# Attention and a quantized gated FFN on one core: the small shift product on GpSimd, and five steps placed elsewhere in the order

## The reference

```
xn  = (x - mean) / sqrt(var + 1e-5)            over the 128 features
out = x + attention(xn) + ffn(xn)

attention: q = xn Wqa Wqb (16 heads of 8), k, v = xn Wkva Wkvb (4 heads of 8), rope on q and k,
           causal softmax(q k / sqrt(8)) v, then Wout and a bias
ffn:       h = silu(Q(xn) Q(Wgate)') * (Q(xn) Q(Wup)'), 352 wide;  Q(h) Q(Wdown)'
Q:         blocks of 16: scale = max|.| / 6, each value rounded to the nearest of
           0, 0.5, 1, 1.5, 2, 3, 4, 6 with its sign, times the scale
```

## Time and profile before

| | |
|---|---|
| median of 3 runs | 790.27 us (788.24 to 791.44) |
| the profiled execution | 788.24 us |
| its span in the profile | 785.8 us |
| TensorE busy | 718.4 us (91%) |
| VectorE busy | 627.7 us (80%) |
| GpSimd busy | 588.6 us (75%) |
| ScalarE busy | 535.9 us (68%) |
| DMA queue | 74.25 MB, 35.1% of 16 engines |
| granted TensorE clock, mean | 0.991 of full speed |

### The profile page before, as it was taken

One profiled execution on the slowest core, in us unless ns is written; L12 is line 12 of the kernel. 1 busy time (PEld: TensorE's weight loads), 2 busy tenths in 40 slices (PEclk: granted clock), 3 DMA queues, 4 the chain that ended last, 5 costly groups with the idle time before them and its releaser, 6 DMA issues.

```text
span 785.8 us, 18291 instructions
## 1 busy us (share of the span) xinstructions
PE 718.4 (91%) x6453; PEld 440.8 (56%) x6453; DVE 627.7 (80%) x1424; ACT 535.9 (68%) x1154; POOL 588.6 (75%) x630
## 2 busy tenths in 40 slices
PE   2467899999999999999999999999999999999886
PEld 1233455665656565665656565665656565665443
DVE  6569888889798888989798888989798888878412
ACT  2213676867777777867777777877777777777772
POOL 4533597878879797868889797878788797856662
PEclk9999899999999999999999999999999999999999
DMA  4432224334334433344334334243334333241111
GB/s 111 108 77 82 67 76 109 93 106 113 99 93 117 103 114 97 94 106 113 97 94 119 104 109 105 89 117 104 96 99 126 94 117 95 77 115 46 57 50 49
DMA packets 84885, 75.41 MB, mean 96 GB/s; under 512 B 28627, under 2 KB 66868, under 8 KB 84796
## 3 DMA queue, kind: packets, MB, share of 16 engines
q1 hardware_dynamic: 84796, 74.25, 35.1%
HBM read 40.38 MB, written 27.25 MB: 86 GB/s over the span
## 4 chain that ended last, share of the span: by engine, by line
PE 62%; DVE 15%; ACT 7%; POOL 6%; issue 4%; DMA 3%; SPq 2%; POOLq 0%; DVEq 0%; ACTq 0%
PE pv_ps L1159 16%; PE exp_ps L1137 12%; PE max_ps L1122 8%; DVE neg_max L732 7%; PE misc_ps L1183 5%; PE max_ps L1123 5%; PE misc_ps L1220 5%; ACT P L958 3%; PE misc_ps L1191 3%; PE misc_ps L1208 3%; PE misc_ps L1218 2%; POOL P L555 2%; PE misc_ps L1169 1%; DVE h_mag L694 1%; PE misc_ps L1187 1%
## 5 line engine op out<-in xcount | busy, mean ns | idle before, releaser
L732 DVE TENSOR_REDUCE neg_max<-max_ps 128x1 f32<-128x512 f32 (+3 forms) x768 | 430.4, 593 | 88.2 <-PE max_ps L1123 86.1
L958 ACT ACTIVATE P<-exp_ps 128x512 f32<-128x512 f32 x512 | 294.7, 599 | 164.0 <-PE exp_ps L1137 163.0
L1137 PE MATMUL exp_ps<-Q,K 128*128 128x512 bf16 (+3 forms) x1024 | 243.4, 301 | 10.2 <-ACT P L958 6.8
L1122 PE MATMUL max_ps<-K,Q 128*128 128x384 bf16 (+2 forms) x768 | 198.9, 278 | 20.1 <-DMA Kd<-K 10.5
L1123 PE MATMUL max_ps<-Kd,Q 128*128 128x128 bf16 x1024 | 190.7, 220 | 1.4 <-DVE neg_max L732 1.2
L555 POOL TENSOR_SCALAR_AFFINE_SELECT P<-P 128x512 f32<-128x512 f32 x256 | 161.7, 667 | 30.6 <-ACT P L961 30.6
L1159 PE MATMUL pv_ps<-P,V 128*32 128x512 f32 (+3 forms) x2048 | 163.9, 438 | 1.2 <-POOL P L555 0.8
L1122 PEld LDWEIGHTS max_ps<-K,Q 128*128 128x128 bf16 x768 | 75.6, 99 | 97.6 <-DVE neg_max L732 53.8
L1123 PEld LDWEIGHTS max_ps<-Kd,Q 128*128 128x128 bf16 x1024 | 99.0, 100 | 42.5 <-issue 22.7
L1137 PEld LDWEIGHTS exp_ps<-Q,K 128*128 128x128 bf16 x1024 | 79.6, 98 | 48.0 <-ACT P L958 26.4
L586 POOL TENSOR_TENSOR h<-gate_sb,up_half 128x352 f32<-128x352 f32 x64 | 59.5, 930 | 54.6 <-DVE gate_sb L745 54.5
(11 more groups left out here) (126 smaller groups left out, 962.7 us busy)
## 6 DMA issues: line engine op xcount, KB each, us to landing
Q<-q_scr SPq DMA_DIRECT2D x64, 224.0 KB
o_scr<-oT SPq DMA_DIRECT2D x31, 256.0 KB, 3.3
q_scr<-q_split SPq DMA_DIRECT2D x16, 384.0 KB, 2.6
Kd<-K SPq DMA_DIRECT2D x64, 96.0 KB
x_in<-x SPq DMA_DIRECT2D x16, 256.0 KB, 4.7
q_scr<-q_split SPq DMA_DIRECT2D x16, 256.0 KB, 2.9
x_res<-x SPq DMA_DIRECT2D x16, 256.0 KB, 5.7
out<-y SPq DMA_DIRECT2D x32, 128.0 KB, 4.4
```

Of the source, the lines that this page charges most:

```text
L732: nc.vector.tensor_reduce(neg_max[:, pr // 4, heads[0]:heads[0] + len(heads), pr % 4, i], max_ps[r % 3][:, 0:len(heads) * n].rearrange("p ...
L958: nc.scalar.activation(P[g % 2][:, hh + r % 2, col:col + 512], ps[:, :], ACT.Exp, scale=SCALE).then_inc(exp_done, 1)
L1122: nc.tensor.matmul(ps[:, col:col + d], Qt, Kt[:, half, g, 0:d], start=True, stop=True)
L1137: last = nc.tensor.matmul(exp_ps[n % 2][:, col:col + width], K[par][:, half, pr // 2, kb * 128:(kb + 1) * 128], Q[par][:, pr, kb * 128:S], ...
```

## The change

The product shift = -mean * rstd moves from VectorE (one instruction with two factors) to GpSimd (one product behind the power). VectorE makes the negative mean beside the variance, as one more instruction, and GpSimd waits for both. Two of the four `bn_stats` go from slot 3 to the end of slot 1; `bn_aggr` and the variance go one reduction earlier and, with the negative mean, behind the fourth reduction of slot 3. x's powers go from behind tile 0 of slot 0 to behind tile 2, and VectorE's magnitudes of x from before the sixth reduction to behind it. h's powers go one place on each: from behind the tiles (2,2), (2,3), (2,4), (3,2) to (2,3), (2,4), (3,2), (3,4). A reduction comes between the two magnitude steps of h. v's first three chunks go one tile on.

```diff
-H_POWERS = [(2, 2), (2, 3), (2, 4), (3, 2)]
+H_POWERS = [(2, 3), (2, 4), (3, 2), (3, 4)]
@@ GpSimd, deviation @@
-                T.wait(pool, var_done, 1, 3, 1)
+                T.wait(pool, var_done, 2, 3, 2)
                 nc.gpsimd.tensor_tensor(rstd[:, :], var_eps[:, :], half_neg[:, :], ALU.pow).then_inc(rstd_done, 1)
+                T.wait(pool, rstd_done, 2, 3, 1)
+                nc.gpsimd.tensor_tensor(shift[:, :], neg_mean[:, :], rstd[:, :], ALU.mult).then_inc(rstd_done, 1)
@@ VectorE, slot 0 @@
                 reduces(0, 4)
+                reduces(0, 5)
                 if T.has(2):
                     T.wait(dve, x_powers, 1, 2, 1)
                     magnitudes(lambda s, n: T.wait(dve, s, 2, 2, n), x_mag[:, :], x_mags)
-                reduces(0, 5)
@@ VectorE, slots 1 and 3 @@
                 reduces(1, 5)
+                if T.has(3):
+                    T.wait(dve, x_loaded, 16, 3, 16)
+                    for c in range(2):
+                        nc.vector.bn_stats(bn_raw[:, c, :], x_in[:, c, :]).then_inc(bn_done, 1)
...
                 invert(T, -1, 1)
                 if T.has(3):
-                    T.wait(dve, x_loaded, 16, 3, 16)
-                    for c in range(NT):
+                    for c in range(2, NT):
                         nc.vector.bn_stats(bn_raw[:, c, :], x_in[:, c, :]).then_inc(bn_done, 1)
                 reduces(3, 2)
                 gated(T, 2)
-                reduces(3, 3)
...
-                reduces(3, 4)
+                reduces(3, 3)
                 if T.has(3):
                     T.wait(dve, mv_done, NT, 3, NT)
                     T.wait(dve, rstd_done, 2, 2, 1)
+                    T.wait(dve, rstd_done, 2, 2, 2)
+                    nc.vector.tensor_scalar(neg_mean[:, :], bn_mv[:, :, 0], -1.0, None, ALU.mult).then_inc(var_done, 1)
                     nc.vector.tensor_scalar(var_eps[:, :], bn_mv[:, :, 1], EPS, None, ALU.add).then_inc(var_done, 1)
+                reduces(3, 4)
                 reduces(3, 5)
@@ VectorE, slot 4 @@
                 reduces(4, 0)
                 if T.has(0):
                     T.wait(dve, h_powers, NT, 0, NT)
-                    magnitudes(lambda s, n: T.wait(dve, s, 2, 0, n), h_mag[:, :], h_mags)
-                reduces(4, 1, 2)
+                    magnitude_bits(h_mag[:, :], h_mags)
+                reduces(4, 1)
+                if T.has(0):
+                    magnitude_floor(lambda s, n: T.wait(dve, s, 2, 0, n), h_mag[:, :], h_mags)
+                reduces(4, 2)
@@ VectorE, before slot 5 @@
-                if T.has(3):
-                    T.wait(dve, rstd_done, 2, 3, 1)
-                    nc.vector.scalar_tensor_tensor(shift[:, :], bn_mv[:, :, 0], -1.0, rstd[:, :],
-                                                   ALU.mult, ALU.mult).then_inc(rstd_done, 1)
@@ ScalarE, extra @@
-                if (slot, r) == (0, 0) and T.has(2):
+                if (slot, r) == (0, 2) and T.has(2):
                     T.wait(act, x_scaled, 1, 2, 1)
@@ TensorE, slot @@
                     values = slot == 3 and T.has(2)
+                    max_tile(T, slot, 4)
                     if values:
                         value_chunk(T, 0)
-                    max_tile(T, slot, 4)
+                    exp_tile(T, slot, 4)
                     if values:
                         value_chunk(T, 1)
-                    exp_tile(T, slot, 4)
+                    max_tile(T, slot, 5)
                     if values:
                         value_chunk(T, 2)
-                    max_tile(T, slot, 5)
```

More of the change, by code:

```diff
@@ L173, in build @@
         rstd = sb("rstd", [128, NT])
+        neg_mean = sb("neg_mean", [128, NT])
         shift = sb("shift", [128, NT])
@@ L685, in scales, with magnitude_bits, magnitude_floor, magnitudes @@
                 nc.vector.tensor_scalar(inv, inv, 1.0 - 2.0 ** -22, None, ALU.mult).then_inc(sem_, 1)
-            def magnitudes(eng_wait, mag, sem_):
+            def magnitude_bits(mag, sem_):
                 m = mag.bitcast(U16)
                 nc.vector.tensor_scalar(m, m, 0x7F80, 0x0040, ALU.bitwise_and, ALU.bitwise_or).then_inc(sem_, 1)
+            def magnitude_floor(eng_wait, mag, sem_):
                 eng_wait(sem_, 1)
                 nc.vector.tensor_scalar(mag, mag, 1.5 * 2.0 ** 22, None, ALU.max).then_inc(sem_, 1)
+            def magnitudes(eng_wait, mag, sem_):
+                magnitude_bits(mag, sem_)
+                magnitude_floor(eng_wait, mag, sem_)
             def weight_scales():
```

## The result

Timed side by side on one chip in 17 executions each, the changed kernel takes 792.36 us in the median (791.19 to 794.79) and the kernel before 789.62 (787.40 to 791.48). The ratio is 1.0037, 95% interval 1.0027 to 1.0047: slower, by 2.7 us. The forecast was 788.6, that is 1.7 less than before. The time lies inside the range (783.5 to 794.5), the sign was wrong. The profiled execution took 792.07 us with a span of 789.8; the one before had 785.8.

A forecast was written before the change was run, and what follows sets the result against it. GpSimd's leg was taken to reach h's transposes last, 0.26 us after TensorE's. Terms -4.1, +2.9 and -0.5 made -1.7 us on the profiled 788.24, 786.5; with 2.0 for the median, 788.6, range 783.5 to 794.5.

The forecast's parts named there:

- The rest: The remaining moves (bn_stats, negative mean, variance, h's powers) cost nothing; in the ramp some 0.3 us either way.
- rival 2: Slot 4: VectorE's bits lose to GpSimd's second selection, TensorE's leg becomes the bound: +4.7 us, 795.0; chance 0.12.
- The two legs and the bound: Slot 3 to slot 7: ScalarE then GpSimd arrives last at h's transposes, TensorE with VectorE 0.26 us sooner.
- a wait of TensorE before h's transposes of 0.5 us or more: Sign of being right, slot 7: TensorE waits longer than now for GpSimd's last step of h.
- x's powers: Slot 0: moved two places on, the 0.29 us gap before the transposes of xn goes, 14 times: -4.1 us.
- The shift: One 128x4 multiply added on GpSimd behind the power costs 0.25 us an iteration, paid in full.
- third rival: GpSimd's multiply costs what the power costs, 1.01 + 0.07 us: +9.1 us, 799; chance 0.04.
- The prediction's other estimate: GpSimd's multiply at twice the least VectorE duration: 0.30 instead of 0.19 us, total 1.4 us more.
- The tile between the magnitude steps: Slot 4: a maximum tile between h's bits and floor, which still hold up GpSimd's selections: -0.03 us an iteration.
- v's chunks: Slot 3: one place on, TensorE leaves the slot about 0.16 us later, on its own leg: nothing by itself.
- The long iteration: At 324.81 bits took 1.01 and delayed reductions once; the new order was to save 0.5 us once.
- Period: Sign of being right: the time of one steady iteration falls from 43.96 to 43.85 to 43.9 us.

The follow-up runs named there:

- e3: The kernel before with only the two bn_stats moved to slot 1: 795.58 us, ratio 1.0065 to the kernel before.
- e1: The changed kernel, but in the ramp iteration t0 = -2 alone all four bn_stats stand in slot 3: 787.78 us, ratio 0.9967 to the kernel before.
- e2: The changed kernel with all four bn_stats in slot 3 in every iteration: 787.72 us, ratio 0.9964 to the kernel before.
- e4: The changed kernel with the load of x for t0 = -2 issued ahead of the constant loads: 787.68 us, ratio 0.9969 to the kernel before.
- e5: e1 with three more 128x4 multiplies behind the shift on GpSimd, into a spare tile: 792.55 us, ratio 1.0041 to the kernel before.
- e8: e1 with GpSimd's last pass over h in two instructions, the first transposes' columns first: 782.52 us, ratio 0.9913 to the kernel before.
- e9: e1 with the shift back on VectorE, without the negative mean: 786.34 us, ratio 0.9950 to the kernel before.
- e7: e1 with v's chunks back at their old place: 787.18 us, ratio 0.9968 to the kernel before.
- e10: e8 with v's chunks back at their old place: 778.69 us, ratio 0.9853 to the kernel before.
- e6: e1 with x's powers on ScalarE back behind tile 0 of slot 0: 791.49 us, ratio 1.0019 to the kernel before.
- e12: e8 with the shift back on VectorE: 786.31 us, ratio 0.9944 to the kernel before.
- e11: e8 with h's two magnitude steps together again, no maximum tile between them: 783.76 us, ratio 0.9914 to the kernel before.

## Why the prediction was wrong, step by step

**The step that failed** is in "The rest": "x's load is issued some 13 us before that place, so it has landed". It is true of the steady part, where `bn_stats` never waits, and I carried it over to the ramp ("In the ramp some 0.3 us either way: nothing") from the steady part alone. In the iteration t0 = -2 the end of slot 1 comes at 20.20 and the load at 24.84, behind SyncE's constants. I had even written what would follow if it had not landed, and gave it no place and no price. It was worth +5.5 us at the second mark; e3 shows the move alone at +5.4, and e1, e2 and e4 take it away by three ways (ratio 0.9967 against 1.0037 for e1, 5.5 us). The steady part's gain then leaves +3.9 at the last mark and +4.0 in span. The sum with this term is -1.7 + 5.5 = +3.8 us; the profiled executions are 3.8 apart (792.07 against 788.24), the medians 2.7. That the time fell inside the range was luck: the range was made for rival 2, which did not set the time.

**The two legs and the bound.** Right in the mechanism. What is added to GpSimd's leg is paid (e5, 0.44 of 0.45), what is taken from it is gained until TensorE's gap is used up (e8 and e9, -0.21 each against a gap of 0.20). What TensorE's leg loses is free until then (e7), and isn't afterwards (e10). One sign was wrong: I named a wait of TensorE before h's transposes of 0.5 us or more, which counts GpSimd's 0.22 and forgets the 0.32 that I had myself put on TensorE's leg. My sum leaves 0.16, measured was 0.20.

**x's powers.** -0.29 an iteration, -4.1 in all: e6 gives 0.33 and 3.7 us. Right.

**The shift.** The multiply was put at 0.19 and is 0.20; with its wait at 0.25, measured 0.26 from start to start. Right, and the power's price (third rival) is excluded. The prediction's other estimate, 0.30 from twice VectorE's least duration, was too high: the pair is 0.20 on GpSimd and 0.14 on VectorE (e12). That it lies on GpSimd's leg is e9's -0.21; e5 shows that what is added there is paid. What I did not see is that a product on VectorE can be held for a whole pass of GpSimd (2.56 us in e9 and e12); in the kernel before no shift took more than 0.69.

**The tile between the magnitude steps.** Put at -0.03. From the selections' start to the power's start it was 371.54 - 368.21 = 3.33 and is 419.59 - 416.28 = 3.31. It falls among the same instructions, as argued; e11 has it at nothing.

**v's chunks.** Nothing in this change, as forecast (e7). The forecast had bits 0.16 later and losing to the second selection; they are 0.22 later against the selections and do lose, 0.88 instead of 0.52. The second rival's mechanism is thus there in nearly every iteration, with 0.88 for the bits in place of 1.01, but TensorE reaches slot 7 still 0.20 ahead of GpSimd, where my sum left 0.16 (0.26 + 0.22 - 0.32). So the rival that I gave 0.12 was not the one that made the kernel slower. Its price was right in kind: once GpSimd's leg is short, e10 has it at 0.59.

**The long iteration.** Put at -0.5, measured -0.75, but that this is what the new order gives is not shown. In the kernel before, the iteration departs from the usual one at a wait of VectorE for the softmax sums, 0.37 at 319.50; then the small instruction for the variance takes 0.99 at 322.71, beside GpSimd's third split of q, and the bits are late. In the changed kernel the same iteration has longer waits (0.76 and 1.11) and is 0.23 too long, e1 has none (43.86 to 43.88 all along but for the iteration behind the second mark), and e6 and e7, with the new order of the steps, have one of 44.94 and 44.74. It comes and goes with that wait.

**Period.** 43.85 to 43.9 was given, 43.85 came; for the ten plain iterations -0.083 each, where the steps make -0.29 + 0.25 - 0.03 = -0.07. The moves of h's powers, `bn_aggr` and the variance, and the negative mean, had no run of their own; this leaves some 0.01 for them together.

In short: every term that repeats held within 0.1 us an iteration, and e1, which has them all and not the ramp's wait, is at 787.78 against 788.6. The sign went by a wait that occurs once, in an iteration that I had not looked at.

## What to carry to other kernels

When a waiting instruction is moved ahead of others on an in-order engine, look up its releaser in the ramp too, iteration by iteration: a load that is issued 13 us early in the steady part may stand behind one-time work in its queue at the start. Before an edit is priced, find the two legs that meet and the gap between them; the same edit (v's chunks here) is worth 0 or 0.59 us an iteration by which leg is longer, so try a neutral edit again after every change of the bound. An iteration that is long once should be followed back to its first wait before an order is credited with curing it. Where two engines share a port, note how far an instruction starts from the other engine's next one; here 0.51 against 0.73 behind a row of 0.60 us pieces decides who waits.

## What the runs showed of the hardware

- A VectorE instruction on 128x4 took 0.14 us in the steady part of e12, 0.67 in the kernel before, and 2.56 in the ramp of e9 and e12, by what GpSimd was doing. In the steady iteration shown it starts at 418.66, and GpSimd's instruction beside it ends by the records at 418.74; it wasn't held, so on GpSimd a recorded end can't be read to 0.1 us as the point from which VectorE can go.
- Multiplies of 128x4 on GpSimd, back to back, stand 0.15 us apart and are recorded as 0.20 for one and 0.51 for three. A power of the same shape is 1.02.
- Bits (128x1408 in 16 bits) take 0.52 in the steady part when they start 0.50 or 0.51 behind the start of GpSimd's selections, 0.91 to 0.95 at 0.66 to 0.69 (once each in e7, e9 and e10), and 0.87 to 0.89 at 0.72 to 0.74; 1.01 at 1.18 in the kernel before. With a reduction between bits and floor, the four selections go with them, 2.97 with 0.52 and 2.68 with 0.88. In e11, with the steps together, it is 2.97 with 0.88.
- TensorE's granted clock in the ramp was lower in the changed kernel by the profile, and its products lasted the same. The window 30 to 40, and one product in it from TensorE's timeline, first the changed kernel, then before:

```profile
30.00:40.00 10.00, 2.41 (x12) 2.28 (x12) 7.25 (x15) 2.69 (x5) 5.70 (x7) 0.50 0.28 89
38.28 1.54 PE L1110 MATMUL max_ps<-ident,w_raw 128*128 128x128 f32 x6 [7.59 <-DVE w_raw L722]
```

```profile
30.00:40.00 10.00, 3.04 (x13) 2.63 (x13) 6.86 (x23) 2.12 (x5) 1.03 (x1) 1.00 0.45 126
32.47 1.54 PE L1097 MATMUL max_ps<-ident,w_raw 128*128 128x128 f32 x6 [7.44 <-DVE w_raw L713]
```

In the changed kernel the grant fell to 0.50, the 1.2 GHz level, while TensorE stood idle for 5.44 us behind the sine product of q (0.69 in the window 26 to 28, 0.50 from 28 on). In the kernel before it stayed at 1.00, the 2.4 GHz level, up to 70 us. Yet the gate and up product, `misc_ps<-wguT,xqT` x4, takes 2.66 in both, at 50.82 and at 45.07, and 1.35 in the steady part of both: near the ends of such idle stretches TensorE was as slow at a grant of 1.00 as at 0.50. So the lower grant shows no cost of its own; the delay was 5.84 us at the sine product and 5.28 at the first mark.
